# A recurrent block and a mixture of experts on one core: unread products in TensorE's waits, and loads, gathers and slot marks moved

## Time and profile before

| | |
|---|---|
| median of 3 runs | 1126.01 us (1123.51 to 1127.64) |
| the profiled execution | 1132.21 us, of which the span of the trace is 1130.2 us |
| TensorE, matmul busy | 1002.5 us, 89% of the span |
| VectorE / ScalarE / GpSimd busy | 789.9 / 547.7 / 680.8 us |
| granted TensorE clock, mean | 0.918 of full |
| chain that ended last | PE 76%, DMA 7%, DVE 7%, issue 5%, ACT 2% |

### The profile page before, as it was taken

How to read it: one execution, slowest core, us unless ns; L and a number is a source line. 1 busy time by engine, 2 the same in 40 slices (tenths; PEclk the granted TensorE clock), 3 DMA queues, 4 the chain that set the end, 5 groups by cost and what they waited for, 6 DMA issues and landing times.

```text
span 1130.2 us, 42039 instructions
## 1 busy us (share of the span) xinstructions
PE 1002.5 (89%) x16550; PEld 817.9 (72%) x16551; DVE 789.9 (70%) x1777; ACT 547.7 (48%) x1120; POOL 680.8 (60%) x1138
## 2 busy tenths in 40 slices
PE   4777999999999999999999998766299999999995
PEld 2546777777777777767867777653289898898894
DVE  3576797877879888768978887161566666666663
ACT  4464685665757766656856866221022222222221
POOL 1077988986888888878879889830123233233321
PEclk9678899988989999989999999585599999999998
DMA  4014033242242242241341341328744454554430
GB/s 100 12 37 82 16 87 87 32 95 52 57 105 56 53 105 54 55 105 30 79 97 30 87 96 24 84 58 277 289 152 166 173 181 150 174 178 146 172 126 4
DMA packets 208622, 111.99 MB, mean 99 GB/s; under 512 B 172364, under 2 KB 191952, under 8 KB 208080
## 3 DMA queue, kind: packets, MB, share of 16 engines
q1 hardware_dynamic: 204720, 101.31, 33.3%
q0 software_dynamic: 3744, 8.40, 2.2%
HBM read 85.42 MB, written 26.08 MB: 99 GB/s over the span
## 4 chain that ended last, share of the span: by engine, by line
PE 76%; DMA 7%; DVE 7%; issue 5%; ACT 2%; SPq 2%; POOL 0%; DVEq 0%; ACTq 0%; POOLq 0%
PE bank L551 20%; PE bank L866 12%; PE bank L879 8%; PE bank L633 6%; PE bank L686 6%; PE bank L641 5%; PE ry L879 4%; PE bank L596 4%; PE ry L714 2%; PE ry L663 2%; DMA scr_n<-arena 2%; PE bank L703 2%; DMA arena<-scr_n 2%; DVE arena L1378 1%; PE bank L584 1%
## 5 line engine op out<-in xcount | busy, mean ns | idle before, releaser
L1787 POOL TENSOR_TENSOR arena<-arena 128x30 f32<-128x30 f32 (+14 forms) x480 | 293.7, 612 | 36.4
L551 PE MATMUL bank<-arena 128*128 128x256 f32 (+2 forms) x992 | 294.2, 438 | 23.5 <-DVE arena L1262 10.1
L1790 POOL TENSOR_TENSOR arena<-arena 128x30 f32<-128x30 f32 (+14 forms) x480 | 285.8, 595 | 37.6
L551 PEld LDWEIGHTS bank<-arena 128*128 128x128 f32 x992 | 188.5, 214 | 79.9 <-issue 37.6
L866 PEld LDWEIGHTS bank<-arena 128*128 128x128 f32 x1248 | 147.5, 194 | 4.5 <-DVE arena L1686 2.6
L866 PE MATMUL bank<-arena 128*128 128x128 f32 x1248 | 148.1, 278 | 2.0 <-DVE arena L1686 2.0
L1378 DVE TENSOR_TENSOR arena<-bank,arena 128x512 f32<-128x512 f32 x128 | 79.4, 682 | 40.9 <-PE bank L633 40.6
L1192 ACT ACTIVATE arena<-arena 128x1 f32<-128x1 f32 x39 | 11.5, 295 | 177.6 <-DVE arena L1650 177.6
L879 PE MATMUL bank<-arena 128*128 x416 | 96.4, 385 | 0.1
L1818 POOL COPY arena<-arena 128x1 int32 (+1 forms) x39 | 7.1, 181 | 146.2 <-DVE arena L1714 146.2
L641 PE MATMUL bank<-arena 128*128 128x128 f32 x576 | 89.7, 296 | 5.3 <-DVE arena L1439 3.3
(11 more groups left out here) (167 smaller groups left out, 1672.2 us busy)
## 6 DMA issues: line engine op xcount, KB each, us to landing
arena<-in_W SPq DMA_DIRECT2D x47, 1024.0 KB, 5.0
scr_n<-arena SPq DMA_DIRECT2D x64, 128.0 KB, 2.8
arena<-scr_n SPq DMA_DIRECT2D x16, 512.0 KB, 4.6
scr_u<-arena SPq DMA_DIRECT2D x16, 512.0 KB, 2.9
arena<-scr_u SPq DMA_DIRECT2D x64, 128.0 KB, 2.9
arena<-in_xTp SPq DMA_DIRECT2D x32, 132.0 KB, 4.0
arena<-in_x SPq DMA_DIRECT2D x64, 64.0 KB, 2.1
scr_x<-arena SPq DMA_DIRECT2D x64, 64.0 KB, 2.9
```

The source lines that it names most:

```text
L551: mm = pe.matmul(ring.tile(m, name)[0:rows, to], lhsT, rhs, start=(i == 0), stop=(i == len(terms) - 1))
L1787: inv_ok.inc(f"m{s}", TT(t, U[:, 0:s, s:s + 1].broadcast_to(shape), U[:, s:s + 1, s + 1:TB].broadcast_to(shape), ALU.mult))
L1790: inv_ok.inc(f"a{s}", TT(U[:, 0:s, s + 1:TB], U[:, 0:s, s + 1:TB], t, ALU.add))
```

## The change

- A function `keep_busy(count)` issues `count` products (the identity, 128 x 128, times 256 columns of the Wo weights) into bank 1, which nobody reads. In body 16 there are 5 after `read_out(15, 1)`, 3 after `centre_y(15)`, 4 after `variance_y(15)` and `turn_x1(14)`; in body 17, 2 after `gates(15)`, 7 after `project_out(15)`, 2 after `turn_x1(15)`; in body 18, 2 after `router(15)`; then 12 after the ranks of the last tiles and 20 after the block table. In all 57.
- `par`, `w_maa1` and `w_maa2` are loaded from ScalarE's DMA queue under a semaphore `first_in`, ahead of everything on ScalarE; only `masks` and `mats` remain in SP's `early`. The engines start on `first_in` and eight constants. `bonus_sum` is made after the first mixing; four loads of activation tables in body -2 go (one is put ahead of the bodies).
- VectorE's `place_known` and all seven `mark_slots` of body 16 now stand after `tokens(14)`, behind both `keep_x_odd`.
- The first half of W2 (experts 0 to 3, four DMAs of 1 MB) is issued after body 15, the second half after body 16.
- The first three gathers take their index straight from the table, without the copy.

```diff
+        idle_ps = banks[1]
...
+        first_in = sem("first_in")
...
-            early = [(par, d["par"]), (w_maa1, ...), (w_maa2, d["maa2"]),
-                     (masks, d["masks"]), (mats, d["mats"].rearrange("m p n -> p m n"))]
+            early = [(masks, d["masks"]), (mats, d["mats"].rearrange("m p n -> p m n"))]
...
-            def load_experts():
+            def load_experts(experts):
...
-                for e in range(E):
+                for e in experts:
...
                 if n + 1 == last:
                     load_routing()
+                if n == last:
+                    load_experts(range(E // 2))
                 if n - 1 == last:
                     load_tokens(last)
-                    load_experts()
+                    load_experts(range(E // 2, E))
...
             def weights(m):
                 if m == 0:
+                    pe.wait_ge(early_in, 32)
...
             def bonus(m):
+                if m == 0:
+                    pe.wait_ge(const_ok, 10)
...
+            def keep_busy(count):
+
+                for _ in range(count):
+                    pe.matmul(idle_ps[:, 0:2 * P], ident, w_sq[:, 3, 0, :], start=True, stop=True)
...
+                if n == last + 3:
+                    keep_busy(2)
                 if has(n - 2):
                     gates(n - 2)
+                if n == last + 2:
+                    keep_busy(2)
...
                     project_out(n - 2)
+                if n == last + 2:
+                    keep_busy(7)
...
                     read_out(n - 1, 1)
+                if n == last + 1:
+                    keep_busy(5)
...
                     centre_y(n - 1)
+                if n == last + 1:
+                    keep_busy(3)
...
                     turn_x1(n - 2)
-            pe.wait_ge(early_in, 80)
-            pe.wait_ge(const_ok, 10)
+                if n == last + 1:
+                    keep_busy(4)
+                if n == last + 2:
+                    keep_busy(2)
+            pe.wait_ge(first_in, 48)
+            pe.wait_ge(const_ok, 8)
...
             route_pe.inc("rank", pe.matmul(late_ps[:, 1], all_ones, oh, start=True, stop=True))
+            keep_busy(12)
...
             route_pe.inc("table", mm)
+            keep_busy(20)
...
         def _(act):
             A = nc.scalar.activation
+            for dst, src in ((par, d["par"]), (w_maa1, ...), (w_maa2, d["maa2"])):
+                act.dma_start(dst, src).then_inc(first_in, 16)
+            nc.scalar.preload_act_table_set("sigmoid_and_others")
...
-                if n < last:
+                if -2 < n < last:
                     sigmoid_tables()
...
-            dve.wait_ge(early_in, 80)
-            for h in range(HALF):
-                nc.vector.tensor_scalar(bonus_sum[:, h, :], head_sum, prm("faaaa", h), None, ALU.mult).then_inc(const_ok, 1)
-            dve.wait_ge(const_ok, 10)
+            dve.wait_ge(const_ok, 8)
+            dve.wait_ge(first_in, 48)
+
+            def bonus_weights():
+                dve.wait_ge(early_in, 32)
+                for h in range(HALF):
+                    nc.vector.tensor_scalar(bonus_sum[:, h, :], head_sum, prm("faaaa", h), None, ALU.mult).then_inc(const_ok, 1)
...
                     token_stats(n - 2)
-                if n == last + 1:
-                    place_known()
-                    mark_slots(0, 3)
                 if has(n - 1):
                     keep_x_odd(n - 1, 1)
-                if n == last + 1:
-                    mark_slots(3, 6)
...
                     mix_stage(n + 2)
+                if n == BODIES[0]:
+                    bonus_weights()
...
                     tokens(n - 2)
                 if n == last + 1:
-                    mark_slots(6, 7)
+                    place_known()
+                    mark_slots(0, KNOWN // GROUP)
...
             def gather(j, s):
-                if not (isinstance(j, int) and j < DEPTH):
+                if isinstance(j, int) and j < DEPTH:
+                    index = table[:, j:j + 1]
+                else:
                     prep.wait(w, j - DEPTH, "zb")
-                idx_ok.inc("gather", nc.gpsimd.tensor_copy(gidx[:, s:s + 1], table[:, bass.ds(j, 1)]))
-                idx_ok.wait(w, j, "gather")
+                    index = gidx[:, s:s + 1]
+                    idx_ok.inc("gather", nc.gpsimd.tensor_copy(index, table[:, bass.ds(j, 1)]))
+                    idx_ok.wait(w, j - DEPTH, "gather")
```

10 lines of the change are left out of this document (6 added, 4 removed).

## The result

The changed kernel takes 1128.37 us (median of 11 runs, 1122.58 to 1134.46), the kernel before 1124.62 us in the same series (1119.59 to 1127.64): ratio 1.0063, 95% interval 1.0035 to 1.0090. A ratio here leaves out the runs more than 1.5% above the fastest of their kernel. The forecast was 1.3 us faster, in a range of 1112 to 1135 that holds the time; the sign was wrong. The profiled execution has a span of 1132.4 us (1130.2 before), TensorE 1024.9 us busy (1002.5), mean clock 0.932 (0.918).

What follows compares the result with a forecast made beforehand. Bounds taken: the start, the solves-to-block-table passage with TensorE mostly at half clock, and the experts' start. Sum -3.2 + 9.7 - 5.3 - 2.5 = -1.3 us, so 1124.7 us at the median, range 1112 to 1135.

Steps and rivals of the forecast that it cites:

- Part 1: Kernel start: first difference of x at 5.1 us instead of 8.3, 3.2 us gained, bounds 2.5 to 3.6.
- I take 5.1: Kernel start: xT's second load assumed to land at 5.1 us, within 4.7 to 5.8.
- Part 2: Last inverse's copy queues behind W2's first half: solves at 764.0, not 752.82; 9.7 us lost together with Part 3.
- first rival: At the last inverse: its copy isn't held up by W2; 1110.6 us, or 1113.9 with a late issue; chance 0.26.
- second rival: Read-out to gates: clock stays at half until the gates, ranks 4.7 us later than before; 1134.7 us; chance 0.17.
- Part 3: Behind the solves: read-out copies follow after 0.8 us in place of 5.2; moved places and marks cost nothing.
- With the stall, which I keep: Read-out: it takes its 4.7 us, including the unexplained stall of 2.53 us.
- some 2 us of room: VectorE behind `tokens(14)`: room left after the moved places and marks before the norm of block 15.
- Part 4: Output chain behind the read-out: fillers hold full clock, 5.3 us gained; 3.0 if the clock returns behind the first five.
- Part 5: Start of the experts: earlier first gather and first rows at full clock, 2.5 us gained, bounds 0.2 to 5.
- First rows at full clock: Experts' first 32 matmuls: 2.2 us and 0.3 at the turn, of which VectorE lets through about 2.0.
- differences are carried to the median: Whole kernel: sum made against the profiled execution, 1132.2 us, then carried to the median of the runs, 1126.0.

Runs made afterwards that it cites:

- w2_back: Changed kernel with all eight loads of W2 behind body 16 again: 1123.33 us, ratio 0.9972 to the kernel before.
- changed_again: Changed kernel without any edit, second execution: 1129.23 us, ratio 1.0031 to the kernel before.
- combined: As w2_after_inverse, with 2 unread products for 5 behind the read-out, 24 for 20 behind the block table, 2 more after the first turn: 1122.90 us, ratio 0.9980.
- changed_third: Changed kernel without any edit, third execution, one run: 1130.50 us.
- w2_half_last: Changed kernel, W2's first half behind body 16, second behind W1; W1 of blocks 1, 2 after first gather; unread products as in combined: 1115.91 us, ratio 0.9929.
- half_last_w1_behind: As w2_half_last, with all of W1 held back until the first gather has landed: 1120.92 us, ratio 0.9947 to the kernel before.
- start_only: Kernel before with only the new first loads, semaphores and table loads at the start: 1120.48 us, ratio 0.9976.
- w2_back_fill28: As w2_back, with 28 in place of 20 unread products behind the block table: 1121.32 us, ratio 0.9973 to the kernel before.
- before_third: Kernel before without any edit, third execution, one run: 1122.43 us.
- w2_after_inverse: Changed kernel with W2's first half issued right behind the four reads of the last inverse in body 16: 1122.88 us, ratio 1.0010.

## Why the prediction was wrong

The parts of the sum, in us, against what the profiles show (the changed kernel less before, from the table above; minus is a gain):

| part | forecast | first profiles | means of three |
|---|---|---|---|
| 1, start | -3.2 | -1.8 | -1.8 |
| 2 and 3, to the end of the read-out | +9.7 | +6.8 | +8.1 |
| 4, to the block table | -5.3 | -5.1 | -3.8 |
| 5, from there on | -2.5 | -0.8 | +0.6 |
| sum | -1.3 | -0.9 | +3.1 |
| recurrence (no term) | 0 | +3.2 | -1.1 |

Against the execution that I read, the sum is off by only 0.4 us, but that is luck: parts 2 and 3 cost 2.9 us less than forecast, since the stall was gone, and parts 1 and 5 gained 3.1 us less. Against three executions of each kernel the sum has the other sign, and that is the sign that the runs have (3.75 us slower by the medians).

**Part 1, first loads: 3.2 us forecast, 1.8 measured** in three profiles (6.5 for 8.3). The step that failed is "I take 5.1" for the landing of xT. The second load has the longer of the two times in the earlier trace rows, 4.3 us, so even in the kernel before it landed at 5.8; that alone leaves 2.5 us. In the changed kernel it took 4.8 us and landed at 6.3, and VectorE started at 6.47. The further 0.6 us go with ScalarE's three loads, which now go out beside it instead of behind it. That these are the cause was not tested by itself.

**Part 2, W2 against the inverse: right.** Solves 11.2 us later was the sum, and 11.2 is the difference in the profiles (18.6 behind GpSimd's last product, 7.4 in w2_back), at half clock, 7.04 us for the 7.3 forecast. The first rival, that the copy passes W2, is refuted by the runs. The page that the prediction cites, the Trainium skill, DMA: Bandwidth & Descriptors, section Queues, rings and completion order, is borne out in both halves. Ring order fits the 7.0 us of the store for 2.6, and its landing at 760.7, behind W2's fourth load. That completion isn't first in, first out, shows in the same place. Of the changed kernel, time to landing of W2's fourth load, issued at 745.4, and of the first load of the tokens, issued behind it at 748.2:

```profile
DMA to landing us min/median/max: 13.4/13.4/13.4
...
DMA to landing us min/median/max: 8.7/8.7/8.7
```

So the tokens landed at 756.9, 1.9 us ahead of the load in front of them (758.8). It did not help the copy. The second rival is refuted too: the clock came back 1.6, 2.9 and 4.1 us behind the read-out's end in the three executions, long before the gates.

**Part 3, slots and read-out.** The read-out starts 0.9 us behind the solves, as forecast. "With the stall, which I keep" failed: the read-out took 1.94 us in all three executions of the changed kernel, for 4.7. I had the solves at half clock and kept a stall that no profile with such solves shows. The "some 2 us of room" for the marks were 0.2 (they end at 782.91, the norm of block 15 starts at 783.12), just enough.

**Part 4, fillers: 5.3 us forecast, 5.1 in the two first profiles, 3.8 between the means of three.** The mechanism held, and the size nearly. The later the clock came back (1.6, 2.9, 4.1 us), the longer the stretch to the block table (27.9, 28.6, 29.2 us), which is the range that I gave for it, 3.0 to 5.3 us gained.

**Part 5, start of the experts: 2.5 us forecast, 0.8 measured in the first profiles, nothing between the means.** The index copy saved 0.2 us. W1 was issued ahead of the gather in all three executions of the changed kernel, where the gather took 5.5 us. In before that was so in the first alone: 6.5 us, for 3.1 and 5.2 in the two others. "First rows at full clock" failed twice over. They ran at half in the first profile, where the twenty had ended 2.4 us ahead of the turn. And where they did run at full clock, in the two others, it was worth nothing. In changed_again, first rows, the copy that VectorE makes for the second block, and the products of the second block:

```profile
805.97 3.84 PE L893 MATMUL bank<-arena 128*128 128x128 f32 x32 [0.52 <-DVE arena L1719]
...
812.08 0.42 DVE L1719 COPY arena<-bank 128x256 f32<-128x256 f32 x1
...
812.55 5.46 PE L893 MATMUL bank<-arena 128*128 128x128 f32 x32 [2.52 <-DVE arena L1719]
```

And the products of the second block in combined:

```profile
809.93 3.84 PE L893 MATMUL bank<-arena 128*128 128x128 f32 x32 [2.51 <-DVE arena L1720]
```

In changed_again the first rows take 3.84 us, and then TensorE waits 2.52 us for VectorE. The second block starts 6.58 us behind the first, for 8.42 at half clock, so VectorE does let 1.8 us through. But the clock is at half in the second block, 0.50 from 813 to 816, and its 32 matmuls take 5.46 us for 3.84, which takes 1.6 back. So it is in changed_third (5.47 us), and in w2_half_last and half_last_w1_behind too; these are the four profiles with more than 307 us behind the second block's start. In combined the clock stays at 1.00 through the same wait of 2.51 us, the second block takes 3.84 us, and the 1.8 us are kept (305.4 us from there on). What decides between the two is open. My "lets through about 2.0" had the wait right and left out the clock behind it.

**The base: the step that turned the sign.** Summed against the one profiled execution, the passage came out 1.9 us longer (9.7 - 5.3 - 2.5) and measured 0.9, 1.6 and 1.4 longer. But "differences are carried to the median" assumed that the median execution has the same passage. It doesn't: 79.2 us in the execution that I read, 73.5 and 74.1 in two others, 70.1 with the same code in start_only. What the change removes (exposed marks of 4.4 us, a stall, gates at half clock), and a gather behind W1, stood all together in that execution; each of the two others lacks some of them. What the change adds is there in each. Against the mean of three, 75.6, the loss is 4.9 us; less 1.8 at the start, some 3 us slower, 0.3%. The times said so beforehand in one respect: the profiled execution was 6.2 us above the median. I shifted it as a whole, where I should have asked which of the savings were in those 6.2 us. Three executions of each kernel are few, with passages of before from 73.5 to 79.2 us, so the 4.9 us are uncertain by some 2.

## What to carry to other kernels

A load that is moved earlier in a queue is paid for by what stands behind it there: here with seven microseconds of late issue and four more of transfer for a store on the critical path, against two gained at the far end. Look for the last order that keeps the critical transfers in front, and move what is needed last behind what is needed first, as w2_half_last does. Products that nobody reads, put into a wait, must end with it: in half_last_w1_behind the wait had become shorter and they outlasted it. And where a forecast is a sum of waits removed, read these waits in more than one execution: additions are there every time, waits are not.

## What the runs showed of the hardware

- A store of 512 KB behind 4 MB of loads and 256 KB of tokens in the same queue took 7.0 us from issue to landing, for 2.6 alone. The issue of the tokens' load ahead of it took 5.45 us, for 1.81: behind the four loads SP itself was held up at the issue. The tokens' first load landed 1.9 us ahead of the 1 MB load issued in front of it.
- TensorE's granted clock fell just behind a gap of 1.9 us between the turn and the first rows, with the engine wholly busy up to the end of the turn (w2_back_fill28: 1.00 in the stretch 796 to 798, 0.53 in 798 to 800), and did not fall over the gap of 0.5 us in changed_again. The length of the gap alone doesn't decide: over a wait of 2.51 us ahead of the second block it stayed at 1.00 in combined, and over one of 2.52 us it fell in changed_again (1.00 in 810 to 812, 0.50 in 813 to 816).
- An indirect gather of 128 rows landed in 3.1 us in five profiles with W1 issued 1.7 us or more behind it (3.9 in w2_back), in 5.1 to 8.0 us with W1 issued just ahead of it, and in 5.2 with W1 issued 0.7 us behind it (before_third).
- TensorE's unexplained stalls amid small products were 0 to 2.5 us in these stages with the DMA engines lightly loaded (3 to 80 GB/s) and 3.0 to 3.9 us with W2 in flight (w2_after_inverse, combined).
